# Early index loads, node scaling in the third layer, selections ahead of window one-hots, and products without a use at the start

## The reference, cut to what matters

```python
h = relu(layernorm(x))
for Wl, b, Wr in three layers:                       # SAGE, relu after the first two
    agg = segment_sum(h[src], dst) / max(count, 1)   # mean over the in-neighbours
    h = agg @ Wl.T + b + h @ Wr.T
x = x + h
h = relu(layernorm(x))
msg = gelu((h[src] + edge_attr) @ We1 + be1) @ We2 + be2
u = (1 + eps) * h + segment_sum(msg, dst)
x = x + gelu(u @ Wu1 + bu1) @ Wu2 + bu2
```

## Time and profile before

| | us |
|---|---|
| median of 3 runs | 973.55 (972.28 to 975.14) |
| the profiled execution | 975.46 |
| its span, first to last instruction | 973.5 |
| PE busy in it | 921.0 |
| PEld, DVE | 700.1, 502.8 |
| POOL, ACT | 379.3, 247.9 |

### The profile page before, as it was taken

The page is one execution under the profiler, slowest core; times in us unless marked ns, Lnnn a source line. Parts: engine busy times, 40 slices in busy tenths (PEclk is TensorE's granted clock), DMA queues, the critical chain, the costliest instruction groups (busy, mean ns, idle before and its releaser), DMA issues.

```text
span 973.5 us, 22393 instructions
## 1 busy us (share of the span) xinstructions
PE 921.0 (95%) x8724; PEld 700.1 (72%) x8724; DVE 502.8 (52%) x1958; ACT 247.9 (25%) x434; POOL 379.3 (39%) x399
## 2 busy tenths in 40 slices
PE   2977999999899999999989999999999999999995
PEld 1734555555545455555679999999998999999994
DVE  6589999995211112112267555543644553644541
ACT  2576677773111011101111111111111111110211
POOL 2000000000000000211178777777777777777772
PEclk9969999999999999999979999999999999999997
DMA  4200011102000000000085434443543444543431
GB/s 135 65 2 12 3 14 13 12 14 65 1 1 1 1 1 1 22 11 12 13 172 158 128 100 133 122 129 95 152 118 96 137 130 108 147 110 106 127 99 32
DMA packets 46832, 68.00 MB, mean 70 GB/s; under 512 B 15268, under 2 KB 25477, under 8 KB 46594
## 3 DMA queue, kind: packets, MB, share of 16 engines
q1 hardware_dynamic: 35202, 42.90, 16.2%
q0 software_dynamic: 11520, 23.62, 9.4%
HBM read 63.18 MB, written 3.30 MB: 68 GB/s over the span
## 4 chain that ended last, share of the span: by engine, by line
PE 84%; DVE 11%; DMA 1%; ACT 1%; issue 1%; SPq 0%; ACTq 0%; DVEq 0%
PE f_ps L1174 25%; PE f_ps L1225 24%; PE f_ps L1279 11%; PE f_ps L1210 9%; DVE f_region L602 2%; DVE f_region L600 2%; PE f_ps L1059 2%; PE f_ps L1052 2%; DVE f_region L606 2%; DVE f_region L604 2%; PE f_ps L1149 2%; PE f_ps L1111 1%; DMA f_rcntT<-in_dst_pt 1%; PE f_ps L1070 1%; PE f_ps L1247 1%
## 5 line engine op out<-in xcount | busy, mean ns | idle before, releaser
L553 POOL DMA_INDIRECT f_adj<-table,f_table_idx x360 | 355.1, 986 | 110.1 <-issue 108.8
L1174 PE MATMUL f_ps<-f_adj,f_parts 125*128 125x500 fp8e4 (+1 forms) x1575 | 331.5, 352 | 0.1
L1225 PE MATMUL f_ps<-f_parts 125*128 125x128 bf16 x4200 | 250.9, 220 | 3.9 <-DVE f_parts L790 3.9
L1225 PEld LDWEIGHTS f_ps<-f_parts 125*128 125x128 bf16 x4200 | 244.3, 98 | 11.0 <-issue 8.6
L1174 PEld LDWEIGHTS f_ps<-f_adj,f_parts 125*128 125x128 bf16 x1575 | 143.6, 97 | 130.0 <-issue 11.1
L538 POOL TENSOR_TENSOR f_rest<-f_region,f_parts 125x512 f32<-125x512 f32 (+1 forms) x7 | 7.3, 1049 | 464.5 <-ACT f_parts L1017 464.5
L929 ACT CAST f_adj<-f_ps 128x500 f32 x213 | 125.9, 591 | 56.8 <-PE f_ps L1059 41.3
L1279 PE MATMUL f_ps<-f_adj 128*128 128x94 f32 (+20 forms) x984 | 128.0, 275 | 3.5 <-ACT f_adj L1039 3.5
L1279 PEld LDWEIGHTS f_ps<-f_adj 128*128 128x128 f32 x984 | 118.3, 192 | 6.0 <-issue 5.9
L770 DVE TENSOR_SCALAR f_adj<-f_iota,f_dst_abs 128x94 f32<-128x94 f16 (+4 forms) x416 | 87.4, 283 | 60.7 <-PE f_ps L1279 60.7
L1210 PE MATMUL f_ps<-f_We,f_region 128*128 128x128 f32 x832 | 115.0, 282 | 0.8 <-DVE f_region L704 0.8
(11 more groups left out here) (135 smaller groups left out, 481.4 us busy)
## 6 DMA issues: line engine op xcount, KB each, us to landing
f_region<-in_edge_attr_T SPq DMA_DIRECT2D x103, 256.0 KB
f_adj<-table,f_table_idx POOLq DMA_INDIRECT x360
f_parts<-in_src_row SPq DMA_DIRECT2D x14, 256.0 KB
f_adj<-inv SPq DMA_DIRECT2D x1, 1562.5 KB
table<-f_region SPq DMA_DIRECT2D x6, 250.0 KB
out<-f_xT SPq DMA_DIRECT2D x6, 250.0 KB, 2.6
f_rcntT<-inv SPq DMA_DIRECT2D x5, 250.0 KB, 3.8
f_xT<-in_xT SPq DMA_DIRECT2D x1, 812.5 KB, 6.3
```

The costliest lines, as they stand in the source:

```text
L553: pool.indirect_dma_start(out=rows[:, r % RW, j * D:(j + 1) * D], out_offset=None, in_=table, in_offset=bass.IndirectOffsetOnAxis(ap=table ...
L1174: ins = pe.matmul(ps[:, dense_ps(i):dense_ps(i) + width(c)], parts[0:NP, (l % 2) * 3 + p, b, :], adj[0:NP, b, lo:hi].bitcast(F8), start=b ...
L1225: ins = pe.matmul(z_ps(g, j), select[0:NP, u % SELECT, j * P:(j + 1) * P], parts[0:NP, 3 + p, b, :], start=b == 0 and j == 0 and p == 0, s ...
```

## The change

- SP loads the first 54 columns of the sources, of both rows of firsts and of the destinations ahead of the other columns. edge_keys for the rest moves from slot 1 to slot 4.
- The memset of c25 goes from POOL to the front of DVE's stream.
- PE computes products that nothing reads (keep_busy): 48 of 128 columns ahead of slot 0, and 5 in each slot that plan.calm names (0 to 7 and 23 to 37).
- The six operations on eps and be2 (split_be2) go into slot CALM, behind check_repeats.
- In layer 3 SP stores and broadcasts 1/std chunk by chunk into rcntT, with a wait between; node_scale of chunks 0 to 4 runs in layer 3's slots, that of chunks 5 and 6 right before the edge groups.
- SP loads source rows and destinations for the edge stage ahead of the table store of the last chunk, once the dense products have ended. DVE makes selections(0) ahead of dst_abs and the window one-hots.
- take_sources waits for POOL's split of the chunk it reads, not for all seven.

```diff
+                if 0 < q < s.NC - 1:
+                    self.put("scale", o + 2, q - 1)
...
+    def calm(self, slot):
+        stats = [t for name, t in self.at if name in ("cent0", "var0")]
+        return slot < min(stats) or max(stats) < slot < min(self.units)
...
-            sp.dma_start(src_idx[0:EP, :], t["src_pt"]).then_inc(idx_in, 16)
-            sp.dma_start(firsts[0:EP, :, :].rearrange("p a n -> p (a n)"),
-                         t["firsts"].partition_broadcast(EP)).then_inc(dst_in, 16)
-            sp.dma_start(dst_idx[0:EP, :], t["dst_pt"]).then_inc(dst_in, 16)
+            sp.dma_start(src_idx[0:EP, 0:HEAD], t["src_pt"][:, 0:HEAD]).then_inc(idx_in, 16)
+            for i in range(2):
+                sp.dma_start(firsts[0:EP, i, 0:HEAD], t["firsts"][i * NT:i * NT + HEAD].partition_broadcast(EP)
+                             ).then_inc(dst_in, 16)
+            sp.dma_start(dst_idx[0:EP, 0:HEAD], t["dst_pt"][:, 0:HEAD]).then_inc(dst_in, 16)
             sp.dma_start(first[:, :], t["tile_first"]).then_inc(first_in, 16)
-            sp.wait_ge(idx_in, 16)
-            sp.wait_ge(dst_in, 32)
+            sp.dma_start(src_idx[0:EP, HEAD:NT], t["src_pt"][:, HEAD:NT]).then_inc(idx_rest, 16)
+            for i in range(2):
+                sp.dma_start(firsts[0:EP, i, HEAD:NT],
+                             t["firsts"][i * NT + HEAD:(i + 1) * NT].partition_broadcast(EP)).then_inc(dst_rest, 16)
+            sp.dma_start(dst_idx[0:EP, HEAD:NT], t["dst_pt"][:, HEAD:NT]).then_inc(dst_rest, 16)
+            sp.wait_ge(idx_rest, 16)
+            sp.wait_ge(dst_rest, 48)
...
             for c in range(NC):
                 b = s.blocks(c)
+                if c == NC - 1:
+                    sp.wait_ge(dense_done, LAYERS * NC)
+                    for i in range(2):
+                        sp.dma_start(src_rows[:, i, :], src_columns(i)).then_inc(src_in[i], 16)
+                    sp.dma_start(dst_tile[:, :], t["dst_tiles"]).then_inc(dst_tile_in, 16)
                 sp.wait_ge(rows_kept, c + 1)
                 sp.dma_start(table[b[0] * NP:(b[-1] + 1) * NP, :].rearrange("(b p) d -> p b d", p=NP),
                              grows[0:NP, c % 2, 0:len(b) * D].rearrange("p (b d) -> p b d", d=D)
                              ).then_inc(rows_out[c % 2], 16)
-            for i in range(2):
-                sp.dma_start(src_rows[:, i, :], src_columns(i)).then_inc(src_in[i], 16)
-            sp.dma_start(dst_tile[:, :], t["dst_tiles"]).then_inc(dst_tile_in, 16)
-            sp.dma_start(inv.rearrange("(b p) -> p b", p=NP), rstd[0:NP, :],
-                         allow_slow_non_contiguous=True).then_inc(rstd_out, 16)
-            sp.wait_ge(rstd_out, 16)
-            sp.dma_start(rstdT[:, :], inv.partition_broadcast(P)).then_inc(rstd_in, 16)
+                sp.wait_ge(agg_kept, 2 * NC + c + 1)
+                sp.dma_start(in_nodes(inv, c).rearrange("(b p) -> p b", p=NP), columns(rstd, c),
+                             allow_slow_non_contiguous=True).then_inc(rstd_out, 16)
+                sp.wait_ge(rstd_out, 16 * (c + 1))
+                sp.dma_start(at(rcntT, c), in_nodes(inv, c).partition_broadcast(P)).then_inc(rstd_in[c % 2], 16)
...
-            pool.memset(c25[:, :], 0).then_inc(eye, 1)
...
+            dve.memset(c25[:, :], 0).then_inc(blank, 1)
             dve.wait_ge(idx_in, 16)
             edge_keys(0, HEAD)
...
-                if slot == 1:
+                if slot == 4:
+                    dve.wait_ge(idx_rest, 16)
                     edge_keys(HEAD, NT)
...
                 if slot == CALM:
                     check_repeats()
...
+                    split_be2()
+                for c in plan.due("scale", slot):
+                    node_scale(c)
...
-            dve.wait_ge(be2_ready, 6)
-            dve.wait_ge(small_in, 16 * 9)
+            for i, b in s.selections(0):
+                select_sources(i, b)
             dve.wait_ge(dst_tile_in, 16)
             dve.tensor_copy(dst_abs[:, :], dst_tile[:, :]).then_inc(abs_ready, 1)
             dve.wait_ge(abs_ready, 1)
             for g in range(OH_AHEAD):
                 window_onehots(g)
-            for i, b in s.selections(0):
-                select_sources(i, b)
+            for c in range(NC - 2, NC):
+                node_scale(c)
             for g in range(END):
...
-                if 3 <= g < 3 + NC:
-                    node_scale(g - 3)
...
+            def keep_busy(n):
+                for _ in range(n):
+                    pe.matmul(ps[:, dense_ps(1):dense_ps(1) + P], ones[:, :], ones[:, :], start=True, stop=True)
+
+            keep_busy(48)
             for slot in range(plan.slots):
                 if slot < GB:
                     sum_group(slot)
+                if plan.calm(slot):
+                    keep_busy(5)
...
                     if i:
                         pe.wait_ge(msg_ready, s.picked[i - 1] + 1)
                     else:
-                        pe.wait_ge(lowest3, NC)
                         pe.wait_ge(rows_kept, NC)
+                if i == 0 and b % s.NBC == 0:
+                    pe.wait_ge(lowest3, b // s.NBC + 1)
```

43 lines of the change are left out of this document (24 added, 19 removed).

## The result

The changed kernel takes 988.37 us in the median of 4 runs (985.32 to 990.06), the kernel before, run beside it, 974.35 (972.28 to 975.57). The ratio is 1.0143, with a 95% interval of 1.0123 to 1.0164: slower, by 14 us where 6.5 were forecast. The profiled execution of the changed kernel is its fastest, 985.32 us with a span of 983.6; it lies 9.9 us above the profiled one of before (975.46), and the spans (983.6 and 973.5) differ by 10.1. What follows splits those 10.1 us.

What follows compares the result with a forecast made beforehand. PE and POOL's unbroken gathers were taken to bound the edge stage, DVE the build. Terms -4.6 - 0.7 + 3.3 + 8.5 = +6.5 us gave 982.0 profiled, 980.0 on the median; range 971 to 987 (own range 976 to 987).

Steps and rivals of the forecast that it cites:

- the string of gathers: Edge stage: POOL's gathers run unbroken from 491.09 us to the last groups, so delaying the first delays the last.
- Early indices: Start: smaller first index loads bring the first one-hot to 7.5 us instead of 12.08, lasting to the dense layers; -4.6 us.
- The quiet slot: Dense layers near 254 us: split_be2 lengthens PE's hole from 2.9 to 4.4 us and may lower the clock; +3.3 us.
- Unused products: Statistics from 24 us: extra PE products keep the clock up and spare part of two slow chunks; -0.7 us.
- Rival C: Build: the unused products at low clock make PE fall behind DVE in 18 slots; up to +6.3 us, chance 0.13.
- The transition: Dense layers to edge stage: SP's wait for returned 1/std starts gathers 10.5 us later, 2.0 given back for stalls; +8.5 us.
- the sign of the string: Near the end: DVE's 2.00 us wait for gathered rows at 952.30, then PE's, taken to show that gathers bound too.
- The term put at nothing: Edge stage start: lowest3 per chunk and window one-hots behind the first selections cost nothing, as the first aggregation awaits gathers anyway.
- Rival A: Transition: SP is held only some 2 us for the small store, table store +2.2; sum -1.8, 971.8 us, chance 0.22.
- Rival B: Edge stage: PE alone ends it, late gathers are absorbed and PE's wait at 496 shrinks by 3; -6.8, 966.8 us, chance 0.15.

Runs made afterwards that it cites:

- the other trace of the same code: Kernel before with only the check of repeats moved from slot 213 + 8 to 213 + 22: 0.9953 on a chip of the second kind.
- best without them: Changed kernel, CALM at 213 + 22, loads and both last tables before one last 1/std return, last scalings in groups 3 and 4, no keep_busy: 0.9944, 1.0028 (second kind).
- the early indices alone: Kernel before with only the split index loads and the keys of the rest in slot 4, c25's memset still on POOL: 971.76 us, 0.9982.
- SP's order alone: Changed kernel with source rows, window indices and last table ahead of chunk 5's 1/std return on SP: 991.44 us, 1.0184; second-kind chips 0.9964, 0.9976.

## Why the prediction was wrong

The direction was right and so was the main event (SP's wait for returned 1/std makes the transition later). The size was too small, and the step that failed is the one from the late first gather to the end: the prediction went by the end of the string of gathers and held the first aggregation's wait for them to be free, where PE ends the kernel and that wait is a new hole of 6.26 us in it.

- **Early indices**, forecast -4.6: the first one-hot came 4.3 us earlier. Right. That it lasts to the dense layers is less sure: at chunk 5 the lead is 6.1 to 6.8 us against the trace of before and 2.4 to 3.2 against the other trace of the same code. The quiet slot then took back clock as well, which the prediction had booked to the split of be2 alone.
- **Unused products**, -0.7: 0.0 and +0.3 at chunk 5 in two of three pairs of kernels, -2.6 in the third (best without them, second trace). The slow passes that the term was built on come in some traces without the products and not in others; with the early indices alone the second pair took 1.00 too. Rival C (they cost) did not come. PE has its hole while DVE computes the rest of the keys, and in the changed kernel the granted clock is 0.50 from 15 to 21 us, as written.
- **The quiet slot**, +3.3 from 1.5 for the operations and 1.8 for the clock: 4.0, from 1.3 and 2.7. The size was right within its range, the second part by luck, for its reason was not. The prediction took the longer hole for the cause, as the hole of 2.9 us had kept the clock before. The same hole lost it in the kernel with the early indices alone. The Trainium skill, "TensorE: Matmul & The Clock Gate", "Why this matters for your kernels", has idle gaps put the clock back to half; here a gap of 2.9 us did so in one kernel and not in another, so the rule gives a risk and not a price.
- **The transition**, +8.5: 12.8. This is the step that failed. The chain on SP was right: after chunk 5's store SP waited 8.9 us for the return (8.5 taken), the last table was issued 14.7 us behind the last dense product (14.3 forecast), the first gather came 20.9 behind it (19). But from there on the sum went by the gathers, "one unbroken string ... what delays their first delays their last", and gave back 2.0 us for a shorter string. The string was shorter by 5.0 us, and that was worth nothing: PE had the bound. The prediction had read PE's wait behind the gather at 952.30 as the sign of the string; that wait, 0.57 us, is in the changed kernel as well (at 964.26), and so are PE's others from 520 us on. By the table above, the profiled executions divide into +5.35 for the later selections (19.15 behind the last dense product against 13.80), +6.26 for the new hole, +1.2 for clock: 12.8. The prediction had the first of these as "PE's selections start later too, by about 3 us" and left it out of the sum.
- **The term put at nothing** is the hole. The prediction says it in its last part: "the first aggregation waits for gathers anyway". In the kernel before that wait is hidden: group 0's sum starts at 501.58 and the first aggregation at 504.14, just as the selections end. With gathers that start 12.3 us later behind the last dense product, and selections only 5.35 later, it becomes a hole. Most of the 6.26 us is this; the smaller part, at most 2.1 by the estimate above, is DVE's hold at the last scaling, whose broadcast waits for a *second* return on SP (from 494.82 to 505.21). The part on node_scale called five of the seven scalings free and did not ask where the other two stand. The kernel with SP's order alone shows that hold by itself, 20.71 us of hole with everything else early.
- Seen from the gathers, the miss is 1.8 us for the first gather (+12.3 where +10.5 was summed), 2.0 for what was given back and did not come, and 0.5 for the rest. A rule that held in this kernel for another reason than the one given is why the forecast came as near as it did.
- **Rival A** (return in some 2 us) fell by the 8.9 us. The Trainium skill, "DMA: Bandwidth & Descriptors", "Where the ~2 µs actually goes", has a small DMA at about 2 us, mostly the receipt of the write, and gives it for the path of DMAs that GpSimd issues, where these come from SP; no wait for a return of 1/std in the changed kernel was under 8 us. **Rival B** had the right engine and the wrong sign: PE alone ends the edge stage, but there the selections were to start 3.0 us earlier and the late gathers to be absorbed, and neither happened.
- The rest of the gap to 14 us, from 10.1 in the profiled executions, is spread between executions: the profiled one of the changed kernel was its fastest, the profiled one of before (975.46) at the slow end of its runs. How it divides between hole and clock in the unprofiled runs was not measured.

## What to carry to other kernels

When a step is moved ahead, list for each of its instances what stands behind it in the queue of every engine it uses, and the last instance first: the first five scalings had a whole chunk of products to hide under; of the last two, one's return stood ahead of the last table on SP and the other's scaling ahead of the first group on DVE. A queue that waits for a store's return should come last in a stage change, behind whatever the next stage starts with. Before naming a string of work as the bound, look whether the engine that ends the kernel ever waits for it; one wait of DVE for a gather was no such evidence, and PE's own waits, the same in all kernels, were. A string that is not the bound can still delay the bound at its start, so ask when its first item is needed as well as its last. A check that runs in a "quiet" slot is only quiet if nobody's operand stands behind it: moving this one brings the last dense product 3.1 us forward in the kernel before and 7.2 in the changed one. How much of it reaches the end was not measured by itself on a chip of the first kind.

## What the runs showed of the hardware that was not expected

- SP's wait for a return did not follow the number of floats stored. In the changed kernel it was 8.9 us for chunk 5's 500 floats behind a table store, and 10.0 for chunk 6's 125 floats behind a broadcast, two source loads, the window indices and a table. With SP's order alone chunk 5's 500 floats took 13.1 (issued at 486.21, the next issue at 499.95), behind the loads and both tables. The stores of 500 floats in stage 1 averaged 6.0. What lies ahead on the queue is a likely cause, but not a full account: 125 floats behind no more than a broadcast still took 8.7 (500.33 to 509.30, less the issue), with gathers running beside them. SP's waits in the changed kernel, all seven chunks:

```profile
SPq L514 <- DMA inv<-f_rstd: 62.1, 7, 10.0
```

- The same hole on PE, 2.89 and 2.90 us, left the granted clock at 1.00 in one kernel and brought it down in another; after holes of 6 us and more PE worked at half speed for another 3.9 to 7.1 us. The first eight products of the first aggregation took 1.94 us there and 1.05 at full clock.
- In the first 30 us the granted clock of the profile and the speed of PE part: a pair of statistics passes took 1.87 us at 24.16 and 1.00 at 38.92, and the kernel before is given 1.00 at both.
- On chips of the second kind the kernel before took 1207 to 1218 us, and the traces of kernels that ran on both kinds agree within 2 us up to the last dense product. The page's row of the selections on PE, busy time, mean, and idle time before them, in the kernel with SP's order alone, first on such a chip and then on the other kind:

```profile
L1267 PE MATMUL f_ps<-f_parts 125*128 125x128 bf16 x4200 | 311.4, 235 | 94.9 <-issue 93.5
```

```profile
L1267 PE MATMUL f_ps<-f_parts 125*128 125x128 bf16 x4200 | 250.0, 220 | 0.9 <-DVE f_parts L832 0.9
```

PE waits 93.5 us for nothing but its own issue, and the clock falls with it (0.90 over the span against 0.975). That the supply of instructions is what is short there is a reading of this row; it was not tested. It is one program on two kinds of chips, and a kernel tuned on one kind can stand in another order on the other: SP's order alone is slower than the kernel before on the one (1.0184) and not slower on the other (0.9964, 0.9976).
